# A fused linear-attention and mixture-of-experts layer: head sums, attention product, weight splits and two loads moved in the hand-written order

## The chip, the cores and the metric

The kernel runs on 1 core of one Trainium2 chip. The metric is the device time of one execution in microseconds (us). The engines are PE (TensorE), DVE (VectorE), ACT (ScalarE), POOL (GpSimd) and SP (SyncE, which here only issues DMAs). Each works through its own list of instructions in order and waits on semaphores.

## What is computed

One layer over 1024 tokens of 256 features, in float32:

```python
xn = layernorm(x)                                  # [1024, 256]
q, k, v = split(xn @ w_qkv)                        # 16 heads of 16
q, k = elu(q) + 1, elu(k) + 1
kv_t   = decay * kv_{t-1}   + k_t * v_t            # decay = sigmoid(decay_param), per head
ksum_t = decay * ksum_{t-1} + k_t
attn = (q * kv / clip(sum_head(q * ksum), 1e-6)) @ w_out
e = argmax(xn @ router_w.T); gate = sigmoid(max logit)
routed = (silu(g * xn @ Wg[e]) * (g * xn @ Wu[e])) @ Wd[e]      # 8 experts, one per token, g = gate
shared = (silu(xn @ Sg) * (xn @ Su)) @ Sd
out = x + attn + routed + shared
```

## The kernel before

Everything is one block with one hand-written instruction list per engine; the order in those lists and the semaphores set the order of the work.

**Front.** SP loads x in four parts (`x_load`, L297) and the q, k and v columns of `w_qkv` (`w_load`, L301). Tokens are normalised in two halves of four tiles (`normalise(n)`, L630 on DVE; `norm(n)`, L450 on ACT), transposed by PE (`transpose_tokens`, L866) and split into a high and a low part of type float32r (`x_hi` L455 on ACT, `x_lo` L636 on DVE). Each weight is split in the same way, so that three matmuls give one float32 product. `qkv_tile(t)` for t = 0..11 makes k, v and q in turn, in PSUM banks t mod 4; ACT (L496, L498) and DVE (L721, L724, L729) read them out. `router_logits(n)` (L877 to L880), `transpose_logits` (L888), `choose`, `ranks` (L895) and `place` make the routing: a row in `sorted_rows` for each token (`s_slot`) and a `plan` of tiles per expert (`s_plan`). POOL then scatters the scaled tokens to `sorted_rows` (L421). The decay is spread from heads to partitions by four small matmuls (L1012).

**Shared expert, first seven parts.** `shared_tile(k, u)` (L289 to L291 from L961) for k = 0..6 makes gate and up parts of the shared expert. ACT applies Silu (L528), DVE multiplies (`hidden(k)`, L772, `s_sh`), and between them DVE does the scans of k (`k_scan`, L741) and q times ksum (`q_ksum`, L756). The weights of the shared gate and up projections come as `sgu` (L312). Their row half 0 is split on DVE (L705, L707) and row half 1 on ACT and POOL (L482, L412).

**Experts.** With this data each of the 8 experts has one tile of 144 token slots, so tile t is expert t. Per tile PE does 16 matmuls of the gate and up projection (L1052), the transposes that bring the tile before back to rows (L990), 16 more of L1052, the transposes of the next tile's rows (L982), and 16 of the down projection (L1068). ACT does L552, L513 and L555, DVE L801 and the copy `yrow` (L793), and POOL stores `yrow` to `sorted_rows` (L429). SP's list does per expert e (`refill(e)`): load the rows of tile t+2 into `xg` (L325, from `rows_of`), then the gate and up weights of expert e+2 into the buffer just freed (`gu`, L340), then its down weights (`dn`, L342). PE's transposes inside tile t need the rows of tile t+1 (`pe.wait_ge(s_xg, 16 * t + 16)`), and PE starts expert e only with its `gu` (`s_gu`).

**Head sums.** The denominator, a sum over each head of q times ksum, goes through seven steps that are laid between the expert tiles: high part (ACT L560), low part (DVE L810), four matmuls per token half (PE L972, L973, `denominators(n, end)`), copy (ACT L564), store and load through HBM to turn it (ACT's queue, L574, L577), reciprocal (DVE L827, L828), a store to HBM that repeats each value 16 times (`rden_rows`, 1 MB, ACT's queue, L580), and two loads back in the spread form (`rspread`, SP's queue, L359). `rspread` has the memory of `ksum`. In the kernel before, denominators 0 are made behind expert 1 and denominators 1 behind expert 2. The scans of kv (L749) and q times kv (L824) also lie between the tiles.

**Tail.** Last shared tile (k = 7), the down projection of the shared expert for 8 token tiles (96 matmuls), then the attention output projection (48 matmuls, `attention_out`, `s_acc`). DVE scales the attention product with `rspread` (L838), ACT makes its high part (L586), DVE its low part (L842). POOL stores the last two expert outputs (L429, L431) and then gathers every token's row (L438) into the memory of `q_sb`. DVE adds gather (L846) and product (L849) to x, and SP stores (L365).

## Time and profile before

| | us |
|---|---|
| median of 3 runs | 138.3 (137.26 to 140.29) |
| the profiled execution | 138.7 |
| its span on the core | 136.8 |

Time line of the span: until 9.4 loads, statistics and the first transposes; to 37.0 the q, k, v tiles and the routing; to 54.5 the shared expert's parts 1 to 6 (part 0 lies between q, k, v tiles 9 and 10); to 110.3 the 8 expert tiles; to 131.0 the tail on PE; to 136.8 the last gathers, additions and stores. PE is busy for 92% of the span.

### The profile page before, as it was taken

To read this page: it belongs to the slowest core of one execution; us is meant where nothing else is said; L and a number is where in the kernel's file an instruction comes from. 1 tells how busy PE (TensorE), PEld (TensorE's weight loads), DVE (VectorE), ACT (ScalarE), POOL (GpSimd) and SP (SyncE) were. 2 spreads that over 40 slices of the span, in tenths; PEclk is the share of its full clock that TensorE was granted. 3 is DMA by queue.
4 is the path that set the end of the run, shared out by engine and by line. 5 is a ranking of instruction groups with operands and counts; after the bars stand their busy time and mean duration, and the time that the engine had idled before them with its cause. 6 is when DMAs were issued, how large, how long until landed. Compare 5 with 4: busy or idle time off the path is not lost.

```text
span 136.8 us, 2550 instructions
## 1 busy us (share of the span) xinstructions
PE 125.7 (92%) x830; PEld 108.0 (79%) x830; DVE 79.2 (58%) x159; ACT 54.2 (40%) x106; POOL 34.3 (25%) x57
## 2 busy tenths in 40 slices
PE   4978879999999998999999999999999999999930
PEld 1244446788888885999889899999999989999920
DVE  0787895894338999993635538374040405952663
ACT  4263888449696836325262222313132221600000
POOL 7603043023876000020202010201020011197830
PEclk9999999999999999999999999999999999999996
DMA  3666999999932101038794977978899284103672
GB/s 95 221 223 119 342 334 213 189 397 400 378 133 77 54 5 29 14 62 296 239 350 155 297 261 184 386 222 316 230 292 349 86 256 141 46 6 109 167 233 103
DMA packets 20052, 27.40 MB, mean 200 GB/s; under 512 B 1336, under 2 KB 16864, under 8 KB 20040
## 3 DMA queue, kind: packets, MB, share of 16 engines
q1 hardware_dynamic: 16232, 22.48, 52.9%
q0 software_dynamic: 1408, 3.58, 8.4%
q10 hardware_dynamic: 2400, 1.19, 2.9%
q8 instruction: 7, 0.11, 0.3%
q14 instruction: 5, 0.04, 0.1%
HBM read 19.90 MB, written 7.34 MB: 199 GB/s over the span
## 4 chain that ended last, share of the span: by engine, by line
PE 46%; DMA 27%; DVE 9%; issue 7%; POOL 6%; SPq 1%; DVEq 1%; ACT 1%; POOLq 0%
DMA sorted_rows<-yrow 15%; PE ps L1052 13%; PE ps L1068 7%; POOL q_sb L438 6%; DMA sgu<-_ffn_shared_gate_up_dram 4%; PE ps L291 4%; PE ps L290 4%; PE ps L289 4%; DMA wqkv<-in_L_attn_w_qkv_dram 3%; PE ps L918 3%; PE ps L924 3%; PE ps L931 3%; DMA q_sb<-sorted_rows,slot_row 3%; DMA x_sb<-in_L_attn_x_dram 2%; DVE yrow L793 2%
## 5 line engine op out<-in xcount | busy, mean ns | idle before, releaser
L1052 PE MATMUL ps<-xgT,gu 128*128 128x144 f32 x256 | 34.1, 286 | 0.7 <-DVE sgu L772 0.7
L1052 PEld LDWEIGHTS ps<-xgT,gu 128*128 128x128 f32 x256 | 32.5, 190 | 1.4 <-ACT xgT L513 1.1
L429 POOL DMA_DIRECT2D sorted_rows<-yrow x8 | 5.6, 699 | 61.1 <-DVE yrow L793 61.1
L801 DVE TENSOR_TENSOR wqkv<-rz,ps 128x288 f32<-128x288 f32 x16 | 7.2, 452 | 23.4 <-ACT rz L552 23.4
L1068 PE MATMUL ps<-wqkv,dn 128*128 128x144 f32 x128 | 17.8, 291 | 0.1
L1068 PEld LDWEIGHTS ps<-wqkv,dn 128*128 128x128 f32 x128 | 16.2, 190 | 0.5 <-DVE wqkv L801 0.3
L552 ACT ACTIVATE rz<-ps 128x288 f32<-128x288 f32 x16 | 6.6, 410 | 23.5 <-PE ps L1052 23.5
L289 PE MATMUL ps<-xT_hi,sgu_hi 128*128 128x512 f32 x32 | 12.8, 399 | 0.0
L291 PE MATMUL ps<-xT_hi,sgu_lo 128*128 128x512 f32 x32 | 12.5, 390 | 0.0
L290 PE MATMUL ps<-xT_lo,sgu_hi 128*128 128x512 f32 x32 | 12.5, 389 | 0.0
L438 POOL DMA_INDIRECT q_sb<-sorted_rows,slot_row x8 | 9.9, 1243 | 4.9 <-POOLq L434 2.7
L793 DVE COPY yrow<-ps 72x512 f32<-72x512 f32 x9 | 6.1, 683 | 8.6 <-DMA sorted_rows<-yrow 8.5
L421 POOL DMA_INDIRECT sorted_rows<-xn,slot_row x8 | 8.7, 1083 | 5.5 <-ACT xn L489 3.7
L918 PE MATMUL ps<-xT_hi,wqkv_hi 128*128 128x512 f32 x24 | 8.2, 420 | 1.2 <-ACT xT_hi L455 0.8
L290 PE MATMUL ps<-wqkv_lo,hT_hi 128*128 128x256 f32 x32 | 9.0, 283 | 0.0
L289 PE MATMUL ps<-wqkv_hi,hT_hi 128*128 128x256 f32 x32 | 9.0, 282 | 0.0
L517 ACT ACTIVATE hT_hi<-sgu 128x512 fp32r<-128x512 f32 x8 | 5.1, 632 | 10.0 <-DVE sgu L772 10.0
L291 PE MATMUL ps<-wqkv_hi,hT_lo 128*128 128x256 f32 x32 | 9.0, 281 | 0.0
L555 ACT ACTIVATE yT<-ps 128x288 f32<-128x288 f32 x8 | 3.3, 412 | 13.0 <-PE ps L1068 13.0
L931 PE MATMUL ps<-xT_hi,wqkv_lo 128*128 128x512 f32 x24 | 7.7, 400 | 0.2 <-DVE wqkv_lo L640 0.2
L924 PE MATMUL ps<-xT_lo,wqkv_hi 128*128 128x512 f32 x24 | 7.6, 396 | 0.0
L996 PE MATMUL ps<-ones 128*128 128x512 bf16 x14 | 5.6, 511 | 1.8 <-POOL ones L373 1.8
(157 smaller groups left out, 228.6 us busy)
## 6 DMA issues: line engine op xcount, KB each, us to landing
gu<-in_L_ffn_w_gate_up_dram SPq DMA_DIRECT2D x8, 1024.0 KB, 6.3
dn<-in_L_ffn_w_down_dram SPq DMA_DIRECT2D x8, 512.0 KB, 6.5
sorted_rows<-zeros SPq DMA_DIRECT2D x1, 2592.0 KB, 17.4
sorted_rows<-yrow POOLq DMA_DIRECT2D x10, 144.0 KB, 4.0
wqkv<-sorted_rows SPq DMA_DIRECT2D x10, 144.0 KB
x_sb<-in_L_attn_x_dram SPq DMA_DIRECT2D x4, 256.0 KB, 3.0
sgu<-_ffn_shared_gate_up_dram SPq DMA_DIRECT2D x1, 1024.0 KB, 6.1
rden_rows<-rden ACTq DMA_DIRECT2D x1, 1024.0 KB, 11.2
```

Source lines behind the costliest of these rows:

```text
L289: nc.tensor.matmul(o, w_hi, m_hi, start=start, stop=False)
L290: nc.tensor.matmul(o, w_hi, m_lo, start=False, stop=False)
L291: return nc.tensor.matmul(o, w_lo, m_hi, start=False, stop=stop)
L421: pool.indirect_dma_start(sorted_rows, bass.IndirectOffsetOnAxis(ap=slot_row[:, i:i + 1], axis=0), xn[:, i, :], None).then_inc(s_scatter, 16)
L438: pool.indirect_dma_start(y_tok[:, i, :], None, sorted_rows, bass.IndirectOffsetOnAxis(ap=slot_row[:, i:i + 1], axis=0)).then_inc(s_gather ...
L793: V.tensor_copy(yrow[:, :, :].rearrange("p j d -> p (j d)"), ps[0:HS, 7, :]).then_inc(s_yrow, 1)
L801: V.tensor_tensor(hr[:, 2 * h:2 * h + 2, :].rearrange("p f s -> p (f s)"), act_sb[:, h, 0:2 * SLOTS], ps[:, 2 * h + 1, 0:2 * SLOTS], ALU.m ...
L918: mm(o, wqkv_hi[:, kc, cols], xT_hi[:, kc, rows], start=(kc == 0), stop=False)
L924: ins = mm(o, wqkv_hi[:, kc, cols], xT_lo[:, kc, rows], start=False, stop=last and kc == KC - 1)
L931: ins = mm(o, wqkv_lo[:, kc, cols], xT_hi[:, kc, rows], start=False, stop=last and kc == KC - 1)
L1052: ins = mm(ps[:, 2 * h + u, (f % 2) * SLOTS:(f % 2 + 1) * SLOTS], gu[p][:, kc, col:col + P], xgT[:, kc, :], start=(kc == 0), stop=(kc == K ...
L1068: ins = mm(ps[:, 5 + c, 0:SLOTS], dn[p][:, f, c * P:(c + 1) * P], hr[:, f, :], start=(f == 0), stop=(f == FC - 1))
```

## The change

SP's list: the v columns are loaded ahead of x parts 2 and 3, where they came behind them. The two `rspread` loads, with their wait for the `rden_rows` store, stand behind `refill(3)`, where they stood behind `rows_of(6)`.

Front: of the first half, tiles 0 to 2 are normalised on DVE and tile 3 on ACT (two and two before). The high part of v is made ahead of that of q. `norm(1)` stands ahead of the decay's exponential. `router_logits(0)` stands ahead of `transpose_tokens(1)`. The decay matmuls stand behind `ranks`, and the decay's copy behind the third q. The high parts of `sgu` are made on ACT inside the q, k, v loop (behind t = 2 and t = 5), the low parts on DVE behind the third q, and `x_lo(1)` stands behind the copy of the first logits. `shared_tile(0, u)` comes behind q, k, v tile 11.

Experts: both halves of the head sums are made behind expert 1 (banks 7 and 4). ACT issues the store of the denominators behind expert 1, their load behind expert 2 and the `rden_rows` store behind expert 3 (before: experts 2, 3 and 5). DVE makes the reciprocal behind expert 3 (before: expert 4). The kv scans 2 and 3 move behind expert 2, and q times kv and the low part of `wout` behind expert 4.

Tail: the product with `rspread` and its high part are made ahead of the last expert, its low part on DVE behind the last expert, ahead of the copy of the last rows. They stood in the tail before.

```diff
@@ SP
             sp.wait_ge(s_x[1], 16)
+            w_load(2, s_wv)
             x_load(2)
             x_load(3)
-            w_load(2, s_wv)
             w_load(0, s_wq)
...
-            for e in range(E - 2):
+            for e in range(4):
                 refill(e)
-            rows_of(6)
-
             sp.wait_ge(s_rdram, 16)
             for c in range(KC):
                 sp.dma_start(rspread[:, c, :].rearrange("p (i t) -> p i t", i=NT),
                              rden_rows.rearrange("(i c p) t -> c p i t", c=KC, p=P)[c]).then_inc(s_spread, 16)
-            rows_of(7)
+            for e in range(4, E - 2):
+                refill(e)
+            for e in range(E - 2, E):
+                rows_of(e)
@@ POOL
-            for h in range(2):
-                pool.wait_ge(s_shi, h + 1)
...
-                pool.tensor_tensor(sgu_lo[:, 1, cols], sgu[:, 1, cols], sgu_hi[:, 1, cols].bitcast(F32), ALU.subtract).then_inc(s_slo, 1)
@@ ACT
-                for i in (n * TH + 2, n * TH + 3):
+                for i in range(n * TH + (3, 2)[n], (n + 1) * TH):
...
+            act.wait_ge(s_wv, 16)
+            A(wqkv_hi[:, :, 2 * D:3 * D], wqkv[:, :, 2 * D:3 * D], ACT.Copy).then_inc(s_whv, 1)
             act.wait_ge(s_wq, 16)
             A(wqkv_hi[:, :, 0:D], wqkv[:, :, 0:D], ACT.Copy).then_inc(s_whq, 1)
...
+            norm(1)
             act.wait_ge(s_dec, 16)
             A(dec_e[:, :], dec_in[:, :], ACT.Exp, scale=-1.0).then_inc(s_dece, 1)
-            norm(1)
             x_hi(1)
-            act.wait_ge(s_sgu, 16)
-            for h in range(2):
-                A(sgu_hi[:, 1, h * F:(h + 1) * F], sgu[:, 1, h * F:(h + 1) * F], ACT.Copy).then_inc(s_shi, 1)
...
+                    if t in (2, 5):
+                        c = t // 3
+                        act.wait_ge(s_sgu, 16)
+                        A(sgu_hi[:, c, :], sgu[:, c, :], ACT.Copy).then_inc(s_shi, 1)
...
             expert_tiles(0, one_)
             qk_high(0)
+            qk_high(1)
             expert_tiles(one_, two)
             den_copy(0)
-            qk_high(1)
-            expert_tiles(two, three_)
             den_copy(1)
             act.wait_ge(s_denc, NH)
             act.dma_start(den_rows.rearrange("(i h) t -> h i t", h=HEADS), den_h.rearrange("h (i t) -> h i t", t=P)).then_inc(s_denst, 16)
-            expert_tiles(three_, four)
+            expert_tiles(two, three_)
             act.wait_ge(s_denst, 16)
             act.dma_start(den[:, :], den_rows).then_inc(s_denld, 16)
-            expert_tiles(four, six)
+            expert_tiles(three_, four)
             act.wait_ge(s_rden, 1)
             act.dma_start(rden_rows.rearrange("(q d) t -> q d t", d=HD), rden[:, :].unsqueeze(1).broadcast_to([NT * HEADS, HD, P])).then_inc(s_rdram, 16)
-            expert_tiles(six, total)
-            gate_silu(LAST)
-            hidden_hi(LAST)
+            expert_tiles(four, seven)
             for c in range(KC):
                 act.wait_ge(s_att, c + 1)
                 A(att_hi[:, c, :], kvsum[:, c, :], ACT.Copy).then_inc(s_atth, 1)
+            expert_tiles(seven, total)
+            gate_silu(LAST)
+            hidden_hi(LAST)
@@ DVE
-            dve.wait_ge(s_sgu, 16)
-            V.tensor_copy(sgu_hi[:, 0, :], sgu[:, 0, :]).then_inc(s_sgh, 1)
-            dve.wait_ge(s_sgh, 1)
-            V.tensor_tensor(sgu_lo[:, 0, :], sgu[:, 0, :], sgu_hi[:, 0, :].bitcast(F32), ALU.subtract).then_inc(s_sgl, 1)
-            x_lo(1)
...
             V.tensor_copy(lrow[:, 0, :], ps[0:2 * E, ROUTE, :]).then_inc(s_lcopy, 1)
+            x_lo(1)
...
             qk_low(0)
+            qk_low(1)
+            expert_tiles(two, three_)
             kv_scan(2)
-            expert_tiles(two, three_)
-            qk_low(1)
             kv_scan(3)
             expert_tiles(three_, four)
...
+            expert_tiles(five, seven)
             dve.wait_ge(s_spread, 16 * KC)
             dve.wait_ge(s_qkv_sum, KC)
             for c in range(KC):
                 V.tensor_tensor(kvsum[:, c, :], kvsum[:, c, :], rspread[:, c, :], ALU.mult).then_inc(s_att, 1)
-            hidden_lo(LAST)
+            expert_tiles(seven, total)
             for c in range(KC):
                 dve.wait_ge(s_atth, c + 1)
                 V.tensor_tensor(att_lo[:, c, :], kvsum[:, c, :], att_hi[:, c, :].bitcast(F32), ALU.subtract).then_inc(s_attl, 1)
+            rows_copy(total)
+            hidden(LAST)
+            hidden_lo(LAST)
@@ PE
-            transpose_tokens(1)
             router_logits(0)
+            transpose_tokens(1)
...
-                if e in (1, 2):
-                    denominators(e - 1, ends[e])
+                if e == 1:
+                    for n in range(NH):
+                        denominators(n, ends[e])
```

## Rows read from the trace of the kernel before

**Rows 1.** The page: busy time of PE, and the ending chain's shares by line.

```profile
PE 125.7 (92%) x830; PEld 108.0 (79%) x830; DVE 79.2 (58%) x159; ACT 54.2 (40%) x106; POOL 34.3 (25%) x57
DMA sorted_rows<-yrow 15%; PE ps L1052 13%; PE ps L1068 7%; POOL q_sb L438 6%; DMA sgu<-_ffn_shared_gate_up_dram 4%; PE ps L291 4%; PE ps L290 4%; PE ps L289 4%; DMA wqkv<-in_L_attn_w_qkv_dram 3%; PE ps L918 3%; PE ps L924 3%; PE ps L931 3%; DMA q_sb<-sorted_rows,slot_row 3%; DMA x_sb<-in_L_attn_x_dram 2%; DVE yrow L793 2%
```

**Rows 2.** Timeline (start us, duration us, then engine, line and work), PE, tile 5.

```profile
90.35 2.12 PE L1052 MATMUL ps<-xgT,gu 128*128 128x144 f32 x16
94.71 0.41 PE L982 MATMUL ps<-ident,wqkv 72*128 72x72 f32 x4
96.97 1.27 PE L1052 MATMUL ps<-xgT,gu 128*128 128x144 f32 x9
```

**Rows 3.** Timeline, SP's queue, tiles 4 to 7.

```profile
88.71 0.37 SPq L325 DMA_DIRECT2D wqkv<-sorted_rows  x1
89.36 0.38 SPq L340 DMA_DIRECT2D gu<-in_L_ffn_w_gate_up_dram  x1
...
108.50 1.00 SPq L359 DMA_DIRECT2D ksum<-rden_rows  x2
110.61 0.37 SPq L325 DMA_DIRECT2D wqkv<-sorted_rows  x1
```

**Rows 4.** The page, DMA issues: count, KB each, median us from issue to landing.

```profile
gu<-in_L_ffn_w_gate_up_dram SPq DMA_DIRECT2D x8, 1024.0 KB, 6.3
rden_rows<-rden ACTq DMA_DIRECT2D x1, 1024.0 KB, 11.2
ksum<-rden_rows SPq DMA_DIRECT2D x2, 512.0 KB, 4.4
```

**Rows 5.** Landing times of the six later gu loads (view of line L340).

```profile
DMA to landing us min/median/max: 5.1/5.9/6.9
```

**Rows 6.** Timeline, the load of the denominators on ACT's queue and its use on DVE.

```profile
84.07 0.36 ACTq L577 DMA_DIRECT2D den<-den_rows  x1
...
89.44 0.23 DVE L827 TENSOR_SCALAR den<-den 128x128 f32<-128x128 f32 x1 [0.25 <-DMA den<-den_rows]
```

**Rows 7.** Windows: length, busy PE, PEld, DVE, ACT, POOL, granted clock, DMA share, GB/s.

```profile
103.00:104.00 1.00, 1.00 (x11) 1.00 (x10) 0.00 (x0) 0.21 (x1) 0.00 (x0) 1.00 1.14 352
131.00:132.00 1.00, 0.05 (x1) 0.00 (x0) 0.90 (x3) 0.00 (x0) 0.38 (x1) 1.00 0.65 176
134.00:135.00 1.00, 0.00 (x0) 0.00 (x0) 0.56 (x2) 0.00 (x0) 0.00 (x0) 0.82 0.32 113
```

**Rows 8.** Timeline of the front, 14 to 22 us.

```profile
14.43 1.28 ACT L477 ACT_TABLE_LOAD   x1
...
17.44 1.09 ACT L455 ACTIVATE xT_hi<-ps 128x512 fp32r<-128x512 f32 x2 [0.53 <-PE ps L866]
...
18.42 1.28 DVE L636 TENSOR_TENSOR xT_lo<-ps,xT_hi 128x512 fp32r<-128x512 f32 x2
...
20.44 0.40 PE L877 MATMUL ps<-xT_hi,rT 128*16 128x512 f32 x1 [0.71 <-DVE wqkv L713]
...
21.99 0.74 PE L918 MATMUL ps<-xT_hi,wqkv_hi 128*128 128x512 f32 x2
```

**Rows 9.** Timeline, start of the expert tiles, and the head sums behind tile 1.

```profile
54.51 2.22 PE L1052 MATMUL ps<-xgT,gu 128*128 128x144 f32 x16 [0.65 <-DVE sgu L772]
...
67.02 1.28 DVE L810 TENSOR_TENSOR att_lo<-ksum,att_hi 128x512 fp32r<-128x512 f32 x2
```

**Rows 10.** Timeline of the tail.

```profile
110.31 0.49 PE L289 MATMUL ps<-xT_hi,sgu_hi 128*128 128x512 f32 x1
...
111.79 0.60 PE L990 MATMUL ps<-ident,yT 128*72 128x128 f32 x4
...
114.45 0.69 DVE L793 COPY yrow<-ps 72x512 f32<-72x512 f32 x1 [5.19 <-DMA sorted_rows<-yrow]
...
126.05 0.42 DVE L849 TENSOR_TENSOR x_sb<-x_sb,ps 128x256 f32<-128x256 f32 x1 [1.43 <-PE ps L291]
...
134.24 0.42 DVE L849 TENSOR_TENSOR x_sb<-x_sb,ps 128x256 f32<-128x256 f32 x1
```

More of the change, by code:

```diff
@@ L181, in build @@
         s_dec = sem("s_dec")
+        s_decp = sem("s_decp")
         s_wk = sem("s_wk")
@@ L545, in _ @@
             hidden_hi(LAST - 1)
-            one_, two, three_, four, six, total = ends
+            one_, two, three_, four, seven, total = ends
             def expert_tiles(begin, end):
@@ L628, in normalise @@
                 V.scalar_tensor_tensor(shift[:, h], mv[:, h, 0], -1.0, rstd[:, h], ALU.mult, ALU.mult).then_inc(s_rstd, 1)
-                for i in (n * TH, n * TH + 1):
+                for i in range(n * TH, n * TH + (3, 2)[n]):
                     V.tensor_scalar(xn[:, i, :], x_sb[:, i, :], mv[:, i, 0:1], rstd[:, i:i + 1], ALU.subtract, ALU.mult).then_inc(s_xn, 1)
@@ L733, in _ @@
                     place()
+                if a == KC:
+                    for h in range(KC):
+                        dve.wait_ge(s_shi, h + 1)
+                        V.tensor_tensor(sgu_lo[:, h, :], sgu[:, h, :], sgu_hi[:, h, :].bitcast(F32), ALU.subtract).then_inc(s_slo, 1)
+                    dve.wait_ge(s_decp, 1)
+                    V.tensor_copy(decay[:, :], ps[:, 7, 256:256 + KC]).then_inc(s_decay, 1)
             def k_scan(a):
@@ L793, in rows_copy @@
                 V.tensor_copy(yrow[:, :, :].rearrange("p j d -> p (j d)"), ps[0:HS, 7, :]).then_inc(s_yrow, 1)
-            one_, two, three_, four, five, total = ends
+            one_, two, three_, four, five, seven, total = ends
             def expert_tiles(begin, end):
@@ L816, in _ @@
             qk_low(0)
+            qk_low(1)
+            expert_tiles(two, three_)
             kv_scan(2)
-            expert_tiles(two, three_)
-            qk_low(1)
             kv_scan(3)
             expert_tiles(three_, four)
-            for c in range(KC):
-                dve.wait_ge(s_kvs, 2 * NH)
-                V.tensor_tensor(kvsum[:, c, :], q_sb[:, c, :], kvsum[:, c, :], ALU.mult).then_inc(s_qkv_sum, 1)
-            expert_tiles(four, five)
             dve.wait_ge(s_denld, 16)
@@ L830, in _ @@
             V.tensor_tensor(sdn_lo, sdn[:, :, :], sdn_hi.bitcast(F32), ALU.subtract).then_inc(s_plo, 1)
-            expert_tiles(five, total)
-            rows_copy(total)
-            hidden(LAST)
+            expert_tiles(four, five)
+            for c in range(KC):
+                dve.wait_ge(s_kvs, 2 * NH)
+                V.tensor_tensor(kvsum[:, c, :], q_sb[:, c, :], kvsum[:, c, :], ALU.mult).then_inc(s_qkv_sum, 1)
             V.tensor_tensor(wout_lo, wout[:, :, :], wout_hi.bitcast(F32), ALU.subtract).then_inc(s_plo, 1)
+            expert_tiles(five, seven)
             dve.wait_ge(s_spread, 16 * KC)
@@ L856, in transpose_tokens @@
             def transpose_tokens(n):
-                for j in range(TH):
+                for j in ((0, 3, 1, 2), (0, 1, 2, 3))[n]:
                     i = n * TH + j
-                    if j < 2:
-                        pe.wait_ge(s_xn, 2 * n + j + 1)
+                    if j < (3, 2)[n]:
+                        pe.wait_ge(s_xn, 3 * n + j + 1)
                     else:
-                        pe.wait_ge(s_xna, 2 * n + j - 1)
+                        pe.wait_ge(s_xna, (1, j)[n])
                     if n and j == 0:
@@ L1004, in _ @@
                 qkv_tile(t)
+            router_logits(0)
             transpose_tokens(1)
-            router_logits(0)
             qkv_tile(3)
             router_logits(1)
-            pe.wait_ge(s_dech, 1)
-            for c in range(KC):
-                ins = mm(ps[:, 7, 64 + c:65 + c], spread[:, c, :], dec_h[:, :], start=True, stop=True)
-            ins.then_inc(s_decp, 1)
             qkv_tile(4)
@@ L1018, in _ @@
             ranks()
-            for t in range(7, 10):
-                qkv_tile(t)
-            for u in range(2):
-                shared_tile(0, u)
-            for t in range(10, 12):
+            pe.wait_ge(s_dech, 1)
+            for c in range(KC):
+                ins = mm(ps[:, 7, 256 + c:257 + c], spread[:, c, :], dec_h[:, :], start=True, stop=True)
+            ins.then_inc(s_decp, 1)
+            for t in range(7, 12):
                 qkv_tile(t)
@@ L1032, in _ @@
             pe.wait_ge(s_plan, 1)
-            for k in range(1, LAST):
+            for k in range(LAST):
                 for u in range(2):
```

35 lines of the change are left out of this document (11 added, 24 removed).

## The prediction

> **What bounds the kernel now.** I read the page first. PE is busy for 92% of the span, and the chain that ended last is mostly PE's own lines, with the DMA of the rows `yrow` at 15% [rows 1]. So time is won only where PE has a gap or in the last gathers, and lost wherever PE is made to wait. The timeline of tile 5 shows the rhythm of the expert tiles: it starts at 90.35 and tile 6 at 96.97, 6.62 us with PE never idle, and the transposes of the next tile's rows start 4.36 us into it [rows 2]. PE has no slack here, but SP has some. Inside tile 4 (83.73, one period before 90.35) it issues the rows of tile 6 at 88.71 and the gate and up weights of expert 6 at 89.36 [rows 3]. The rows are needed at 94.71, the weights at 96.97. With the median landing of 6.3 us [rows 4] the weights are there at 95.7, 1.3 us early. That is all the slack there is on SP's list.
>
> Then I read three gaps. In the front PE waits before the second logits at 20.44 [rows 8]. Before the first expert tile it waits 0.65 us for the product on DVE [rows 9]. At the end the copy of the last rows waits until 114.45 for a store of `yrow` [rows 10], and the gathers behind it finish after PE's last matmul, which the windows place at 131.05 [rows 7].
>
> **Front and shared expert: 2.0 us gained.** Two `sgu` splits leave DVE ahead of `x_lo(1)`, which starts at 18.42 although its input is there about 18.0, half of the two copies that start at 17.44 [rows 8]. The v weights come earlier, so q, k, v tiles 1 and 2 lose two short waits, about 0.6 us by my reading of the same timeline. Against that, `norm(1)` now stands ahead of the table load. That load is 1.28 us [rows 8] and was hidden in a wait; now ACT does norm(1) to about 15.6, the load and the exponential to 17.1, and only then `x_hi(1)`, 0.3 us earlier than 17.44. The second logits then start near 19.1 instead of 20.44, and the fourth q, k, v tile, relieved of the decay matmuls too, near 20.3 instead of 21.99. The decay matmuls (0.3 to 0.5 us) come later on PE, so 1.4 us are left. The low parts of `sgu` (about 1.2 us each) end near 33.2 on DVE, just as PE wants them. DVE reaches `hidden(0)` about 2.8 us earlier, since its list is ahead of PE's by then, and the wait of 0.65 us before tile 0 [rows 9] goes as well. Sum: 1.4 + 0.65 = about 2.0; tile 0 starts at 52.5 instead of 54.51. Bounds: 1.0 (if a split or the table load is late) and 2.8 (if all of DVE's lead reaches PE).
>
> **Head sums: 0.6 us lost.** PE does the same 8 matmuls, now in one place. Their low parts are four operations instead of two in a row on DVE, 0.64 us each; the first two begin at 67.02 and end at 68.30 [rows 9]. The second pair lets PE's second half begin only 1.3 us later, where its first half takes 0.9. With tile 1's later part unchanged relative to the others I get a start of tile 2 of 69.05, and tile 3 at 75.7 instead of 77.11: 1.4 us early, no longer 2.0. Bounds 0.2 and 1.3. ACT's extra high parts (2 x 0.57) lie beside PE's matmuls in tile 1.
>
> **SP's list: 7.2 us lost.** This is the main term. Write S4, S5, S6 for the starts of tiles 4 to 6. Without a stall they are 82.3, 88.95 and 95.57. ACT issues the load of the denominators behind tile 2, 0.34 us into tile 3 (84.07 against 83.73 in the kernel before [rows 6]). It takes 5.3 us (89.44 is its use), DVE needs 1.2 us for maximum and reciprocal, and ACT issues the `rden_rows` store at S4 + 0.4 = 82.7. That store took 11.2 us [rows 4]. It ran beside the weights of expert 7, issued in the 1.4 us before it, with the DMA engines full at 352 GB/s [rows 7]. In the new place it meets the same company, expert 5's weights, less one load of rows, so I take 10.7: it lands at 93.45. Until then SP stands at its wait. Behind it are queued the rows of tile 6 and both weights of expert 6. Then come the two `rspread` loads (1.0 us of issue) and, 2.11 us after them as in the row pair 108.50 and 110.61 [rows 3], the rows of tile 6, issued at 95.6; the weights follow 0.65 us later [rows 3], at 96.2. The rows must be there at 93.3. 1.05 MB of `rspread` and 0.15 MB of rows at about 350 GB/s, with 1.4 us to start, land at 98.9. The gate and up weights, 1.05 MB more, land at 102.0 (issue plus 5.8, between the 5.1 and 6.9 of [rows 5]).
>
 The rest of tile 5 (96.97 less 94.71, 2.26 us) then takes up to 4.5 and ends by 103.4, against 101.2 at the full clock. I take 102.8 for the start of tile 6, between 102.0 (the weights alone) and 103.4. The loss is 102.8 less 95.57, 7.2 us. Later tiles are served in time, since SP is then ahead of PE.
>
> The Trainium skill ("TensorE: Matmul & The Clock Gate", section on the HAM clock gate) says that an idle array is put back to half its rate and has to work for a while before it is let go. The rows agree on the fall; no row here shows the way back up. By that rule alone the sum would stand nearer its upper end, by 0.6 us.
>
> The loss could be smaller. The nearest row for 1 MB in the same 512 B pieces with little beside it is the load of `rspread`, 4.4 us for each half [rows 4]. If the store took 4.9 us, the weights of expert 6 would be issued 5.8 us earlier and the loss would be 1.2 us. That is the lower bound; the upper is 9, with the weights of expert 6 at 6.9 us and the low clock through tile 6.
>
> The Trainium skill ("DMA: Bandwidth & Descriptors", "Queues, rings and completion order") has descriptors of one issuing queue consumed in ring order on each engine. No row here shows it apart. If it didn't hold, the rows of tile 6 could pass `rspread` and PE could go on about 0.6 us sooner, but the weights would still set tile 6.
>
> **Tail: 2.25 us gained.** Count from the end of tile 7 (110.31). The store of `yrow` that held the last copy until 114.45 [rows 10] ran beside the `rspread` loads issued at 108.50. These are gone from here. The copy then needs only the transposes that start at 111.79 and last 0.60, so it starts near 112.3, 2.15 us earlier, also with the two low parts of the product (2.35 us) ahead of it on DVE, which end near 111.5. The gathers shift by as much, and then DVE's additions set the end: the first product is added at 126.05, two additions of 0.42 us a token tile make some 0.86 with what lies between, so the eighth is at 132.1 instead of 134.24 [rows 10]. Tile 7's own wait (0.1) goes too. Bounds: 0 and 2.4.
>
> **Sum.** -2.0 + 0.6 + 7.2 - 2.25 = +3.55 on the profiled execution's 138.7, so 142.25. That execution is 0.4 above the median, so I predict 142.0.
>
> **Rivals.**
>
> *The store lands in time (faster).* Place: SP's wait for `rden_rows`. If the store landed within 3.8 us of its issue, SP would lose nothing, the first, second and fourth terms give -3.65 and the time is 134.7. It is still faster by over 2% while the loss is under 0.9 us, a store of up to 4.7 us. For it: the store has its place where only one expert's weights are in flight, and its share of the engines is small. Against it: the only row says 11.2 us beside the same transfers. Chance 0.17.
>
> *A partial block (within 2%).* With a store of 5 to 9.5 us, or a clock that stays up and weights that land quickly, the loss is 1 to 6.4 us and the time 135.6 to 141. The threshold is near: 10.7 us against about 9.7. Chance 0.30.
>
> *The tail gains nothing.* If the copy of the last rows, now behind `att_lo`, or the gathers stay where they are, the loss is 5.8 and the time 144.2. For it: three operations stand ahead of that copy now. Against it: they end before PE's transposes. Chance 0.13.
>
> *The forecast,* loss of 6.5 us or more on SP's list with the tail gained: 0.40, its own range 141 to 143.5.
>
> Under about 2% a measurement of this kernel can't be told from no change. So faster 0.17, within 2% 0.30, slower 0.53. The range that leaves out 2 in 10 goes from 137.0, inside the partial block, to 144.5.
>
> **What would show it.** Right: SP's `rspread` issues stand at about 93 and the rows of tile 6 at about 95; PE has one gap of 5 to 6 us inside tile 5, released by that load, with a granted clock of 0.5 at its end; tile 6 waits for its weights or runs its way there at the low clock; tile 0 starts near 52.5; from the end of tile 7 to the end of the span it takes 24.2 instead of 26.5. Wrong: the `rden_rows` store lands in under 9 us, or PE has no gap over 3 us among the expert tiles, or the second logits start no earlier than before.

## The result

| | us |
|---|---|
| the kernel before, median of 4 | 138.5 (137.26 to 140.29) |
| the changed kernel, median of 4 | 142.5 (141.38 to 144.54) |
| ratio, with its 95% interval | 1.030 (1.018 to 1.042) |
| profiled execution of the changed kernel, and its span | 142.35, 140.3 |

The changed kernel is slower, by about what was forecast (142.0; range 137.0 to 144.5). The interval begins below 1.02, so from these runs alone a loss of over 2% is likely but not certain; on another chip the ratio was 1.048 (1.038 to 1.058), which is dealt with below. Medians are over all executions; every ratio, here and below, leaves out those that ran over 1.5% above the fastest of their kernel.

The waits of PE in the changed kernel, from 50 us to the end (line, releaser, total us, times, longest):

```profile
PE ps L973 <- DMA wqkv<-sorted_rows: 5.9, 1, 5.9
PE ps L1039 <- DMA gu<-in_L_ffn_w_gate_up_dram: 0.2, 1, 0.2
```

The kernel before had one such wait there, 0.7 us for DVE. L973 (L982 before) is the transposition of the next tile's rows; L1039 is L1052 of before and L1055 is L1068. The timeline of SP's queue answers [rows 3]:

```profile
79.86 0.38 SPq L339 DMA_DIRECT2D gu<-in_L_ffn_w_gate_up_dram  x1
81.07 0.37 SPq L341 DMA_DIRECT2D dn<-in_L_ffn_w_down_dram  x1
91.14 1.00 SPq L356 DMA_DIRECT2D ksum<-rden_rows  x2
93.74 0.39 SPq L324 DMA_DIRECT2D wqkv<-sorted_rows  x1
94.40 0.38 SPq L339 DMA_DIRECT2D gu<-in_L_ffn_w_gate_up_dram  x1
```

For 9.7 us SP issues nothing. The rows of tile 6 go out at 93.74; in the rhythm of [rows 3] (4.98 us into the tile) they would have gone at 86.2. PE's timeline, tile 5 and the start of tile 6, against [rows 2]:

```profile
90.37 2.13 PE L1039 MATMUL ps<-xgT,gu 128*128 128x144 f32 x16
98.42 0.74 PE L973 MATMUL ps<-ident,wqkv 72*128 72x72 f32 x4 [5.93 <-DMA wqkv<-sorted_rows]
98.95 4.00 PE L1055 MATMUL ps<-wqkv,dn 128*128 128x144 f32 x16
102.79 1.39 PE L1039 MATMUL ps<-xgT,gu 128*128 128x144 f32 x10
```

and the windows there (columns as in [rows 7]; the one behind the busy times of PE, PEld, DVE, ACT and POOL is the granted clock):

```profile
94.00:95.00 1.00, 0.00 (x0) 0.00 (x0) 0.00 (x0) 0.00 (x0) 0.00 (x0) 1.00 1.15 346
95.00:96.00 1.00, 0.00 (x0) 0.00 (x0) 0.00 (x0) 0.00 (x0) 0.00 (x0) 0.93 1.19 370
96.00:97.00 1.00, 0.00 (x0) 0.00 (x0) 0.00 (x0) 0.00 (x0) 0.00 (x0) 0.50 1.07 396
...
101.00:102.00 1.00, 1.00 (x6) 1.00 (x6) 0.00 (x0) 0.00 (x0) 0.00 (x0) 0.50 1.12 249
102.00:103.00 1.00, 1.00 (x7) 1.00 (x7) 0.00 (x0) 0.01 (x1) 0.00 (x0) 0.66 0.94 328
103.00:104.00 1.00, 1.00 (x10) 1.00 (x9) 0.00 (x0) 0.41 (x1) 0.00 (x0) 1.00 1.03 418
```

Where the 3.5 us of span (136.8 to 140.3) come from, by the starts of the tiles (us):

| | before | changed | this step adds |
|---|---|---|---|
| tile 0 | 54.51 | 52.06 | -2.45 |
| tile 3 | 77.11 | 74.26 | -0.40 |
| tile 5 | 90.35 | 87.97 | +0.47 |
| tile 6 | 96.97 | 102.79 | +8.20 |
| end of tile 7 | 110.31 | 115.94 | -0.19 |
| end of the span | 136.8 | 140.3 | -2.13 |

### The profile page after: what moved, and what is told of

Read it like the earlier page. It is cut to its first block, busy times and chain, and to the rows that moved or that the text cites. A ratio compares the mean times of both kernels' runs of the same rounds, so it can differ in the third digit from the quotient of the medians.

```text
span 140.3 us, 2550 instructions
## 1 busy us (share of the span) xinstructions
PE 126.5 (90%) x830; PEld 110.2 (79%) x830; DVE 79.1 (56%) x160; ACT 53.8 (38%) x105; POOL 30.0 (21%) x55
## 4 chain that ended last, share of the span: by engine, by line
PE 71%; DMA 14%; DVE 7%; ACT 3%; issue 1%; SPq 1%; POOL 1%; DVEq 0%; ACTq 0%; POOLq 0%
PE ps L1039 14%; PE ps L1055 10%; PE ps L289 9%; PE ps L288 9%; PE ps L290 9%; DMA rden_rows<-rden 5%; DMA den<-den_rows 5%; PE ps L987 4%; DMA wqkv<-sorted_rows 3%; PE ps L912 3%; PE ps L925 3%; PE ps L918 3%; PE ps L981 2%; DVE xT_lo L632 2%; PE ps L973 2%
## 5 line engine op out<-in xcount | busy, mean ns | idle before, releaser
L1039 PE MATMUL ps<-xgT,gu 128*128 128x144 f32 x256 | 34.1, 287 | 0.2 <-DMA gu<-in_L_ffn_w_gate_up_dram 0.2
L1039 PEld LDWEIGHTS ps<-xgT,gu 128*128 128x128 f32 x256 | 32.4, 190 | 0.8 <-issue 0.4
L1055 PE MATMUL ps<-wqkv,dn 128*128 128x144 f32 x128 | 19.2, 308 | 0.0
L1055 PEld LDWEIGHTS ps<-wqkv,dn 128*128 128x128 f32 x128 | 18.0, 208 | 0.0
L973 PE MATMUL ps<-ident,wqkv 72*128 72x72 f32 x36 | 4.1, 238 | 5.9 <-DMA wqkv<-sorted_rows 5.9
L433 POOL DMA_INDIRECT q_sb<-sorted_rows,slot_row x8 | 7.7, 966 | 4.9 <-POOLq L429 2.7
L973 PEld LDWEIGHTS ps<-ident,wqkv 72*128 72x128 f32 x36 | 3.7, 149 | 6.3 <-DMA wqkv<-sorted_rows 6.1
```

The source lines that it names most:

```text
L433: pool.indirect_dma_start(y_tok[:, i, :], None, sorted_rows, bass.IndirectOffsetOnAxis(ap=slot_row[:, i:i + 1], axis=0)).then_inc(s_gather ...
L973: ins = tr(ps[:, bank, col:col + HS], xg[:, j, c * P:(c + 1) * P], ident[0:HS, 0:HS])
L1039: ins = mm(ps[:, 2 * h + u, (f % 2) * SLOTS:(f % 2 + 1) * SLOTS], gu[p][:, kc, col:col + P], xgT[:, kc, :], start=(kc == 0), stop=(kc == K ...
L1055: ins = mm(ps[:, 5 + c, 0:SLOTS], dn[p][:, f, c * P:(c + 1) * P], hr[:, f, :], start=(f == 0), stop=(f == FC - 1))
```

## The experiments

The kernels are called e1 to e12 here, after the beginning of their labels, and go in the order of the questions. Two theories stood against each other. **SP's list:** the wait for the `rden_rows` store holds rows and weights back, and PE's gap follows the landing of that store. **The company:** the 2 MB of store and load cost PE time among the weights wherever they stand. Later it was also asked what the low clock costs and whether the tail's gain is real.

**The wait moved back by two experts (e1), by one (e2).**

```diff
-            for e in range(4):
+            for e in range(E - 2):
                 refill(e)
             sp.wait_ge(s_rdram, 16)
...
-            for e in range(4, E - 2):
-                refill(e)
```

In e2 the two ranges are `range(5)` and `range(5, E - 2)`.

> The changed kernel with one edit: the wait for the rden_rows store and the two rspread loads stand behind refill(5) on SP's list. Theory (SP's wait holds back the rows of tile 6 and the weights of expert 6): the gap of 5.9 us and the low clock go, tiles 5 to 7 take 6.62 us each, the span falls by the 8.2 us that tile 5 has over that, to about 132, and the time is about 134.3, 0.97 of the kernel before. Rival (the other moves cost the time, ACT and DVE being late between the tiles): little changes, 141 to 143.

> The changed kernel with the wait and the two rspread loads one expert later, behind refill(4). Theory: the rden_rows store landed 3.2 us into tile 5, where the rows of tile 7 are due about 5 us in, so SP's wait costs the rows nothing; the gate and up weights of expert 7 come behind 1 MB of rspread and land near the start of tile 7, with up to 1 us of wait for PE. Time 134.3 to 135.5. Rival (what counts is that 1 MB of rspread and the weights meet on the DMA engines, wherever SP issues them): over 138.

e1 took 143.1 us, ratio 1.022 (1.019 to 1.025), where 134.3 us and 0.97 were expected. In tile 5 waits of 0.7 us for the rows and 0.5 for the weights are left of the gap of 5.9, and the tile takes 8.3 us instead of 14.8. So SP's wait was the cause of the gap, but another wait came. DVE, then PE:

```profile
107.28 2.36 DVE L828 TENSOR_TENSOR kvsum<-kvsum,ksum 128x1024 f32<-128x1024 f32 x2 [4.91 <-DMA ksum<-rden_rows]
```

```profile
111.57 4.21 PE L1053 MATMUL ps<-wqkv,dn 128*128 128x144 f32 x16 [3.26 <-DVE wqkv L793]
```

The product with `rspread` now stands ahead of the last expert on DVE. The loads are issued from 97.63 on and land up to 9.2 us later, behind the weights of expert 7, so DVE stands for 4.91 us, with the last tile's products queued behind it, and PE waits 3.26 and falls to the low clock again. (This profiled execution took 145.6, 2.5 us over the median; only the waits are read from it, not its tail.) The store met the weights of two experts instead of one and took 14.5 us instead of 7.6. That alone isn't shown to be the reason: in e6 below, with the same list on SP, it took 8.1.

In e2 the store took 15.0 us, SP still waited for 9.5, and the gap stood in tile 6 (3.84 us, for the rows of tile 7). Its times lay between 140.2 and 145.7, too wide for a ratio. Both expectations had the loads cost PE at most 1 us in a later place; both missed. Each of the runs shows the wait wherever something needed soon stands behind it: on SP's list in e2, on DVE's in e1.

**The product back in the tail (e6).** e1 and, in addition, the product and its high and low parts where they were before:

```diff
@@ DVE
-            expert_tiles(five, seven)
+            expert_tiles(five, total)
+            rows_copy(total)
+            hidden(LAST)
             dve.wait_ge(s_spread, 16 * KC)
             dve.wait_ge(s_qkv_sum, KC)
             for c in range(KC):
                 V.tensor_tensor(kvsum[:, c, :], kvsum[:, c, :], rspread[:, c, :], ALU.mult).then_inc(s_att, 1)
-            expert_tiles(seven, total)
+            hidden_lo(LAST)
             for c in range(KC):
                 dve.wait_ge(s_atth, c + 1)
                 V.tensor_tensor(att_lo[:, c, :], kvsum[:, c, :], att_hi[:, c, :].bitcast(F32), ALU.subtract).then_inc(s_attl, 1)
-            rows_copy(total)
-            hidden(LAST)
-            hidden_lo(LAST)
```

On ACT the two high parts stand behind `hidden_hi(LAST)`.

> The changed kernel with the two rspread loads and their wait behind refill(5), and with the product with rspread, its high part and its low part back in the tail as in the kernel before; front, head sums and reciprocal stay early. Theory that the order 'product ahead of the last expert' is what turns late rspread loads into a wait of PE: no PE gap over 1 us in the tiles 5 to 7, tile 7 ends near 108.3, the tail takes 25 to 26.5, ratio 0.975 (0.965 to 0.985). Rival, that any place of these loads ahead of the last tile costs PE time by contention with weights and rows alone: ratio 0.99 to 1.01, with waits for rows and weights adding to over 2 us.

138.95 us, ratio 0.984 (0.973 to 0.996), just inside the expected 0.965 to 0.985, though the interval reaches into the rival's 0.99 to 1.01. PE's waits decide between them. From 50 us on they are down to

```profile
PE ps L1036 <- DVE sgu L765: 0.5, 1, 0.5
PE ps L1052 <- DVE wqkv L793: 0.2, 1, 0.2
```

and the tiles end at 109.62. The loads are hardly earlier than in e1 (issued from 96.71 on, landing after 7.5 and 8.7 us). So it was the product ahead of the last expert that made the late loads cost PE time in e1. The same kernel prices the company: the store and the loads run beside the weights of three experts, and tiles 3 to 6 take 27.51 us (75.58 to 103.09) where four times 6.62 is 26.48, 1.0 us in all.

**The changed kernel on that chip (e5), with a quarter of the store (e7), and without the new front (e8).**

e7 changes the store on ACT's queue to 4 of the 16 repeats; the other 12 are zeros that SP's queue writes behind `wout`, so the attention part of its output is wrong, and only its time is of use. e8 has the diff's edits below "Experts" and "Tail" and of the `rspread` loads, and none of the front.

```diff
-            act.dma_start(rden_rows.rearrange("(q d) t -> q d t", d=HD), rden[:, :].unsqueeze(1).broadcast_to([NT * HEADS, HD, P])).then_inc(s_rdram, 16)
+            act.dma_start(rden_rows.rearrange("(q d) t -> q d t", d=HD)[:, 0:4, :], rden[:, :].unsqueeze(1).broadcast_to([NT * HEADS, 4, P])).then_inc(s_rdram, 16)
```

> The changed kernel once more, beside the others on one chip. Both theories: ratio to the kernel before 1.03; one PE gap of 5 to 6 us inside tile 5, tile 6 starting near 102.8, and from the end of tile 7 to the end of the span 24 to 25 us. If the late start of the product additions that the kernels with the moved wait showed on their chip (first addition 3.65 us behind PE's first attention matmul) is the chip's, it appears here too; if it comes from the moved loads, it does not.

> The changed kernel with the rden_rows store cut to 4 of its 16 repeats (0.26 MB); the rest of the buffer is filled with zeros long before, so the attention part of the output is wrong and 0.79 MB of store are left out beside the expert tiles. Theory (SP's list stands until the store has landed, tile 6 follows the landing): the store lands within 4 us of its issue near 83, SP's wait ends by 87.5, where SP comes to it anyway near 87.3, PE has no gap over 1.5 us inside tile 5, tile 6 starts 5 to 8 us earlier than in the changed kernel, ratio 0.97 to 0.985. Rival (the two rspread loads and the rows behind them cost PE the time whatever the store does): a gap of 3 us or more remains and the ratio stays above 1.0.

> The changes of the expert part and the tail alone; the front is that of the kernel before. Theory that the parts add: tile 0 starts at 54.5 as before, everything after it is as in the changed kernel, so ratio 1.045 to 1.05 (the changed kernel's 1.03 plus 2.4 us or 1.7%). Rival, that the front's gain is eaten by the block because the store meets other transfers: ratio 1.03, tile 6 starting at 102.8 although tile 0 starts 2.4 us later.

On this chip the kernel before took 141.9. The changed kernel took 148.6, ratio 1.048 (1.038 to 1.058); e7 144.9, ratio 1.023 (1.013 to 1.033); e8 150.1, ratio 1.060 (1.049 to 1.071). The changed kernel was expected at 1.03 again, with a gap of 5 to 6 us and a tail of 24 to 25: its store took 11.4 us here instead of 7.6, the gap was 7.9 and the tail 27.3. PE's timeline of e5, then of e7:

```profile
101.66 0.74 PE L973 MATMUL ps<-ident,wqkv 72*128 72x72 f32 x4 [7.90 <-DMA wqkv<-sorted_rows]
102.19 4.14 PE L1055 MATMUL ps<-wqkv,dn 128*128 128x144 f32 x16
106.12 2.15 PE L1039 MATMUL ps<-xgT,gu 128*128 128x144 f32 x14
```

```profile
97.58 0.74 PE L977 MATMUL ps<-ident,wqkv 72*128 72x72 f32 x4 [4.27 <-DMA wqkv<-sorted_rows]
98.11 4.14 PE L1059 MATMUL ps<-wqkv,dn 128*128 128x144 f32 x16
102.04 1.17 PE L1043 MATMUL ps<-xgT,gu 128*128 128x144 f32 x4
```

and the `rspread` issues on SP, e5, then e7:

```profile
94.35 1.00 SPq L356 DMA_DIRECT2D ksum<-rden_rows  x2
```

```profile
90.65 1.19 SPq L360 DMA_DIRECT2D ksum<-rden_rows  x2
```

The issue comes 3.7 us earlier, PE's gap is 3.6 us shorter, and tile 6 starts 3.6 us earlier (4.08, less the 0.52 by which tile 0 is earlier). That is the dose and the answer, one for one: the gap follows the landing. It does so between the chips too: the time from the start of tile 5 to the `rspread` issue is 1.96, 3.17, 5.12 and 5.53 us in e7, the changed kernel's first trace, e5 and e8, and the gap is 4.27, 5.93, 7.90 and 8.10. What I had expected of the small store itself was wrong: 0.26 MB took 6.8 us, not 4. With the weights of expert 5 issued 2.7 us ahead, a quarter of the bytes does not make a quarter of the time; in e8, with the full store as far behind them, it took 10.7. The rival's numbers (a gap of 3 us or more, a ratio above 1.0) came true, and one part of it with them, since a part of the gap is left: the rows are issued 2.36 us behind the first `rspread` issue and land 4.6 us later, behind 1 MB of `rspread`. The other part, that the store doesn't matter, did not. For no gap at all the store would have had to land another 4.3 us earlier, 2.5 us behind its issue; this is an estimate from the one-for-one relation.

In e8 tile 0 starts at 54.80, in e5 at 53.17; the medians differ by 1.6 us. So the front's gain is kept through the block, about as the sum had it. The ratio is above the expected 1.045 to 1.05 because that was reckoned from 1.03 for the changed kernel.

**The front alone (e4).** The SP move of the v weights and all edits of the part "Front", nothing else:

> The kernel before with only the front of the change: v ahead of x parts 2 and 3, three tiles normalised on DVE, high part of v first, norm(1) ahead of the table load, logits 0 ahead of the transposes, decay matmuls and the splits of the shared weights moved. Experts and tail as before. Theory: the first expert tile starts 2.4 us earlier and nothing takes it back, so 136.1 (0.982). Rival (the gathers and the DMAs of the tail give it back): 137.5 or more.

138.7 against 140.2 us on its chip, ratio 0.988 (0.986 to 0.991), a gain of 1.6 us, less than the expected 2.4. Tile 0 starts at 52.77, 1.74 earlier than at 54.51 in the first trace of the kernel before. A part of the rival may be in it, for its tail takes 28.2 us against 27.6 in the other trace of the kernel before (e9), but these two are from different chips.

**PE kept busy in the gap (e3 with 24 matmuls, e11 with 36).** Ahead of `transpose_sorted` in tile 5:

```diff
+                    if e == 5:
+                        for _ in range(24):
+                            mm(ps[:, 5, :], ones[:, :], ones[:, :].unsqueeze(1).broadcast_to([P, 4, P]), start=True, stop=True)
```

> The changed kernel with 24 matmuls of 128x512 bf16 ones into the free bank 5 ahead of the transposes of the next rows in tile 5, which PE runs (5.2 us) while it would be idle. Nothing else changes. If the low clock sets the start of tile 6, the rest of tile 5 takes 2.3 instead of 4.4 us and tile 6 starts up to 2.1 us earlier: time 140.5 to 141.5. If the weights of expert 6 set it (issue 94.40, landing 5.5 to 7.8 us later), the time falls by less than 1 us. In both cases the granted clock stays at 1.00 through tile 5.

> The changed kernel with 36 extra bf16 128x512 matmuls on PE in tile 5, 8.0 us by the 0.222 us each that 24 of them took, ahead of the transposes that wait for the rows of tile 6; their result is not used. They should fill the gap of 5.9 to 7.9 us. Theory that the low clock behind the gap costs about 2 us (L1055 at 4.00 instead of 2.17): granted clock 1.00 all through tiles 5 and 6, L1055's group of 16 takes 2.2 us again; if the weights of expert 6 are there, the time is that of the changed kernel less 2 us plus what the extra matmuls outlast the gap (0 to 2 us). Rival, that the low clock costs nothing because tile 6 waits for its weights anyway: tile 6 starts on the landing of gu of expert 6 with a wait of 1.5 us or more, and nothing is won.

e3 took 146.8 us (ratio 1.042) and met neither of its two forecasts: the 24 ended 2.82 us before the rows came, and the clock fell all the same, later and for less long. From the transposes to tile 6 it takes 3.77 us, between the two values that follow. In e11 (ratio 1.035) they filled the gap, and the granted clock was 1.00 in every window from 92 to 106:

```profile
93.65 7.93 PE L1051 MATMUL ps<-ones 128*128 128x512 bf16 x36
101.42 0.42 PE L973 MATMUL ps<-ident,wqkv 72*128 72x72 f32 x4
101.68 2.17 PE L1058 MATMUL ps<-wqkv,dn 128*128 128x144 f32 x16
103.69 2.14 PE L1039 MATMUL ps<-xgT,gu 128*128 128x144 f32 x16
```

From the transposes to tile 6 it is 2.27 us here and 4.37 in the changed kernel, and tile 6 doesn't wait for its weights in either. In the changed kernel the view of the one `gu` load issued at 94.40 says when they came:

```profile
DMA to landing us min/median/max: 6.3/6.3/6.3
```

They were there at 100.7, just when PE would have wanted them at the full clock (98.42 + 2.27 = 100.69) and 2.1 us before it got to them. So the clock, not the weights, set tile 6 there, and the low clock costs 2.1 us. The time of e11 (145.4 us) gives no second reading of that price, for the changed kernel was not run on its chip.

**The repetition moved from the store to the loads (e10), and the quarter store with the old loads in the same place (e12).** Both have the wait behind `refill(4)`.

```diff
-            act.dma_start(den_rows.rearrange("(i h) t -> h i t", h=HEADS), den_h.rearrange("h (i t) -> h i t", t=P)).then_inc(s_denst, 16)
+            act.dma_start(den_rows.rearrange("(h i) t -> h i t", h=HEADS), den_h.rearrange("h (i t) -> h i t", t=P)).then_inc(s_denst, 16)
...
+            act.dma_start(rden_rows[0:P, :], rden[:, :]).then_inc(s_rdram, 16)
...
+                sp.dma_start(rspread[:, c, :],
+                             rden_rows[0:P, :].rearrange("(c h i) t -> c h (i t)", c=KC, i=NT)[c].unsqueeze(1).broadcast_to([HEADS // KC, HD, NT * P])).then_inc(s_spread, 16)
```

> The changed kernel with the repetition moved from the store to the loads: rden is stored once (64 KB instead of 1 MB), with the token tiles of a head side by side, and the two rspread loads read each head's 4 KB row 16 times; they stand behind refill(4). Theory (late rspread is the only fault of the new order): the store takes 4 to 7.6 us like the store and load of den, SP waits at most 2 us, rspread lands by 98, no PE gap over 1 us inside the expert tiles, the product is made ahead of the last expert without a wait, the tail takes 24.3 us; front -2.4, head sums -0.4, tail -2.2 add to -5.0: ratio 0.965 (0.955 to 0.975). Rival (loads among the weights cost PE time wherever they stand, as rows behind them in the same queue land late): waits for rows or weights of 1.5 to 4 us remain, ratio 0.98 to 1.0.

> The changed kernel with the rden_rows store cut to 4 of its 16 repeats as in the run with the quarter store (0.79 MB left out beside the expert tiles, the rest of the buffer zeros, so the attention part of the output is wrong), and with SP's wait and the two rspread loads, which read 1 MB in pieces of 512 B as in the changed kernel, behind refill(4). Theory (the new order fails only by when the store is done and by what stands behind it on SP's list; the small store's kernel failed by loads that read the same rows again and again): the store lands near 91, SP waits 1 to 2 us at a place where it has slack, rspread lands within 8 us of its issue, no PE gap over 1 us in tiles 5 to 7, the product is ready before the last expert, ratio 0.965 to 0.98 (0.98 if the product additions start late as on the last two chips). Rival (1 MB of rspread loads behind refill(4) delays the rows and weights of expert 7 in the same queue by itself, as 18 us of landing in the small store's kernel suggest): rows of tile 7 land over 8 us behind their issue at 94, PE waits 3 us or more in tile 6, ratio 1.0 or more.

e10 was to be the best version and took 148.0 us, ratio 1.047 (1.033 to 1.061), beyond its rival's 0.98 to 1.0 too; the profiled execution took 148.1. Its store landed in 5.1 us and SP issued `rspread` at 89.55 with no wait. But the loads ran on and on. The timelines of PE and DVE:

```profile
108.36 0.74 PE L973 MATMUL ps<-ident,wqkv 72*128 72x72 f32 x4 [6.29 <-DMA wqkv<-sorted_rows]
```

```profile
107.52 2.36 DVE L830 TENSOR_TENSOR kvsum<-kvsum,ksum 128x1024 f32<-128x1024 f32 x2 [4.01 <-DMA ksum<-rden_rows]
```

`rspread` was there 18 us after its issue, and the rows of tile 7, issued at 93.88 behind it, 14.5 us after theirs; tile 6 had already waited 1.75 us for its weights. Between 96 and 104 the DMA share was 0.90 to 1.16 at 140 to 272 GB/s; in [rows 7] it was 1.14 at 352. Reading each row 16 times in this form, 18 us, is dearer than writing it 16 times (7.6 to 15.0 us for the store in these runs). The Trainium skill ("DMA: Bandwidth & Descriptors", "Rules for kernel authors") has a rule that an outermost dimension under 16 keeps a DMA to at most that many engines; the source's is 8 here. The trace fits it: in the last two windows before `rspread` was there, 106 to 108, the DMA share was 0.54 and 0.53, about half of the 16 engines. No run here separates that from the repeated reads.

e12 keeps the place and has the old loads (like e7 it leaves out 12 of the repeats, and its output is wrong in the attention part): 139.6 against 141.6 us, ratio 0.986 (0.978 to 0.994). `rspread` lands in 6.9 and 9.7 us, and PE's waits behind 50 us are 0.7 for DVE, 0.7 in two parts for weights, 0.5 for rows and 0.4 and 0.3 for others, none over 1. So the place is sound once the store is done by 90.5, and e10 failed by the form of its loads. It isn't free: tile 6 takes 8.05 us instead of 6.62, and tiles 3 to 7 together 35.1 where five times 6.62 is 33.1. The expected 0.98 had the late product additions, which follow, already in it; those 2.0 us it did not have.

**The tail.** The kernel before once more, for its trace:

> The kernel before once more, for its trace beside the others on this chip. If the late start of DVE's product additions (first addition up to 3.65 us behind PE's first attention matmul, against 0.92 in the first two traces) is the chip's or the execution's, it can appear in this trace too; if it comes from the moved product, it never appears in the kernel before.

140.9 us, where the runs of the kernel before beside it have a median of 140.4. From the end of tile 7 to the end of the span:

| | tail, us | first product addition behind PE's first `attention_out` matmul, us |
|---|---|---|
| before, changed (first chip) | 26.5, 24.4 | 0.92, 0.92 |
| before (e9), front alone (e4) | 27.6, 28.2 | 0.92, 0.92 |
| product in the tail (e6) | 26.9 | 1.50 |
| changed (e5) | 27.3 | 3.88 |
| e2, e3, e7, e8, e10, e11, e12 | 27.0 to 27.5 | 3.63 to 4.07 |

In the first pair of traces the tail is 2.1 us shorter, as forecast. Where one chip has both orders, the new one is 0.5 and 0.6 us shorter (e10 and e11 against e9), 1.0 us shorter (e2 and e3 against e4) and 0.4 us longer (e5 against e6). The addition of e5, on DVE:

```profile
138.25 0.42 DVE L844 TENSOR_TENSOR x_sb<-x_sb,ps 128x256 f32<-128x256 f32 x1 [8.38 <-PE ps L290]
```

The additions start some 3 us late and are then the end. In most of these traces PE shows an idle time of 0.3 to 0.7 us put down to "issue" (nothing that the profile shows) just ahead of it. The first addition is late in all nine other traces of kernels with the product ahead of the last expert, but not in the changed kernel's first one. And it isn't the moved product that does it, for e6, with the product in the tail, waits 2.1 us at the second addition, and the kernel before has such waits too, at later additions. In e9, on DVE:

```profile
130.91 0.42 DVE L849 TENSOR_TENSOR x_sb<-x_sb,ps 128x256 f32<-128x256 f32 x1 [2.11 <-PE ps L291]
```

It is the third product addition; the second and fourth wait 0.80 and 0.71 us for PE. In e4 the fourth waits 1.22 us for PE and the fifth 1.85 us for something that the profile doesn't name. The first trace of the kernel before has no such wait behind the first addition. So PE's results reach DVE late in every trace but the first two, whatever the order. In the new order it is the first addition that is hit, and with it all the others. The cause of the delay is open; no run here takes it apart.

## Why the prediction was right, and where its sizes were off

**Front.** Forecast -2.0, measured -2.45 (e4 alone: -1.74 at tile 0). The second logits start at 18.89 (forecast 19.1), the fourth q, k, v tile at 19.80 (20.3), tile 0 at 52.06 (52.5). The steps hold in order (ACT's `x_hi(1)` comes at 16.43, 0.7 us before the forecast). One of them holds on some traces only: the wait of [rows 9] before tile 0 is gone in the first trace, in e3 and in e11, but in the eight others with the new front 0.4 to 0.7 us of it is left. In e4 it is 0.50 of the 0.71 us by which the front is worth less.

**Head sums.** Forecast +0.6, measured -0.4. This term had the wrong sign and lay outside its bounds (0.2 and 1.3). The low parts, L804, and the second pair of matmuls, L963:

```profile
64.08 2.49 DVE L804 TENSOR_TENSOR att_lo<-ksum,att_hi 128x512 fp32r<-128x512 f32 x4
```

```profile
66.22 0.40 PE L964 MATMUL ps<-att_lo,head_r 128*16 128x512 f32 x1
66.72 0.39 PE L963 MATMUL ps<-att_hi,head_r 128*16 128x512 f32 x1
```

The low parts begin at 64.08, 5.38 us into tile 1, and end at 66.57. So PE loses 0.27 us at the second pair, where I had it lose 0.4 and kept the other waits of this stretch. In [rows 9] the low parts begin 5.79 us into tile 1, behind a copy that waited for a store. That wait is missing in the changed kernel's first trace. It isn't the earlier front that removes it, for the front alone has it. The copy in the kernel before, then in e4:

```profile
66.05 0.69 DVE L793 COPY yrow<-ps 72x512 f32<-72x512 f32 x1 [1.77 <-DMA sorted_rows<-yrow]
```

```profile
64.36 0.69 DVE L787 COPY yrow<-ps 72x512 f32<-72x512 f32 x1 [1.82 <-DMA sorted_rows<-yrow]
```

The ten other traces with both head sums behind expert 1 have it too, with 1.2 to 1.8 us. Why the first one lacks it is open; it was luck for the time. From tile 0 to tile 3 the first two traces have 22.60 (before) and 22.20 us; on the other chips the old order takes 22.74 (e9) and 22.65 (e4), and the new one 22.6 to 23.1. There the term is between -0.2 and +0.4, nearer to the forecast.

**SP's list.** Forecast +7.2, measured +8.2 in tile 5, plus 0.47 in tiles 3 and 4, where PE waited 0.21 us for the weights of expert 4. Place, mechanism and order of the links were as forecast; e1 and e7 show the place and the mechanism. Several durations were off and nearly cancelled. The load of the denominators took 7.6 us instead of 5.3, so the store was issued at 83.48 and not 82.7. The store took 7.6 us, not 10.7, and landed at 91.14, 2.3 us ahead of the forecast:

```profile
74.60 0.36 ACTq L572 DMA_DIRECT2D den<-den_rows  x1
...
83.48 0.60 ACTq L575 DMA_DIRECT2D rden_rows<-rden  x1
```

```profile
82.24 0.23 DVE L817 TENSOR_SCALAR den<-den 128x128 f32<-128x128 f32 x1 [2.52 <-DMA den<-den_rows]
```

From there the rows were issued 2.6 us later (forecast 2.15) and landed after 4.7 (3.3). That the rows take so long behind 1 MB of `rspread` was under-priced by 1.4 us. So with the store at 7.6 us I would have forecast a partial block, and measured a full one. "The store lands in under 9 us" was even one of the signs that were to show the forecast wrong, and it came true; the threshold of about 9.7 us for the store was misplaced. The rival's "lands within 3.8 us and SP loses nothing" should by e7 have read 2.5 us. That rival and the lower bound of 1.2 us also come out only with 6.3 us for the landing of the weights, where the sum takes 5.8; measured were 6.3.

The late issue and the short store are hardly two errors of their own. In eight traces no further weights are issued before the full store lands: before, e9 and e4, the changed kernel, e3, e5, e8 and e11. The store is issued 1.4 to 3.6 us behind the gate and up weights there, and it lands 11.2 to 13.4 us behind those weights: 95.94, then 97.31 plus 11.2 in the kernel before; 79.86, then 83.48 plus 7.6 in the changed one. So its landing goes by the issue of those weights more than by its own, and a store issued later takes less time. That is a pattern over traces, which no run here tests; the forecast's own 12.1 us (1.4 and 10.7) lies inside it.

The Trainium skill ("DMA: Bandwidth & Descriptors", "Queues, rings and completion order") has each engine consume descriptors in ring order, though a later one may finish its write first. The traces agree with the order: in the changed kernel, e5, e7, e10 and e12 the rows land behind the `rspread` loads issued before them, most plainly in e10, where they needed 14.5 us.

**The clock.** Forecast: tile 6 at 102.8, between weights (102.0) and clock (103.4). It started at 102.79, but by the clock alone, 2.1 us by e11; the weights were there at 100.7. The Trainium skill ("TensorE: Matmul & The Clock Gate", its section on the HAM clock gate) has the array work for a while before its rate comes back, and this trace shows it: PE resumes at 98.42, the granted clock averages 0.66 in 102 to 103 and is 1.00 after.

**Tail.** Forecast -2.25, measured -2.13, by the steps named: the copy of the last rows waits 1.01 us, for PE, instead of 5.19 for a store [rows 10]. The eighth product addition comes 6.02 us behind the first, as worked out. On other chips the gain is between -0.4 and 1.0, for the open reason above. The rival "the tail gains nothing" is nearer to that in size but not in cause: the copy and the gathers moved forward as forecast, and what came late were PE's results.

The forecast of 142.0 thus came out of a sum in which -1.0 (head sums), -0.45 (front), +1.5 (SP's list with tiles 3 and 4), +0.1 (tail) and -0.2 (tile 7) nearly cancel. The mechanism and the main term were right; that the sum came within 0.6 us of the median is luck. The other chip's 1.048 is the same mechanism at another size: the store took 11.4 us, PE's gap was 7.9, and the tail was only 0.4 us shorter than that of e9.

**What is better than both kernels.** The product in the tail with the loads behind `refill(5)` (e6, 0.984) and the front alone (e4, 0.988). Their intervals overlap.

## What to carry to other kernels

A wait in a list of DMA issues costs what stands behind it: put it after the last transfer that an engine needs soon, and then ask which engine's list now holds the early consumer of the late data, for it can cost as much there. Moving work out of a tail pays only if its operand is there; if it isn't, the tail's wait becomes a wait in the middle, and that one also costs the clock. And a transfer's time is that of its company and its moment: one row of the trace prices it for one place only.

## What was not expected of the hardware

- A gap of 5.9 us on PE cost 8.0: 5.93 of waiting and 2.1 of low clock behind it (e11). The low level lasted about 6.8 us.
- The same 1 MB store in pieces of 512 B took 7.6 to 11.8 us in the eight traces with one expert's weights beside it, and 8.1, 14.5 and 15.0 us with two; a quarter of it took 5.6 and 6.8 us.
- Two loads that read 4 KB rows 16 times each, 1 MB in all, were done 18 us after their issue, against 4.5 us for each half from separate rows in the changed kernel and 6.9 and 9.7 us in the same place (e12), and held up all that was behind them.
- In the twelve traces of e1 to e12, but not in the first pair, DVE waited up to 3 us longer for PE's last results, in the old order and in the new, and the profile doesn't say why.
